# Evenly spread projection matmuls and an earlier path for the softmax reciprocals in a gated cross-attention kernel

## The chip, the cores and the metric

The kernel runs on one core of a Trainium2 chip. The metric is the device time of one execution in microseconds (us). A core has a matmul engine (PE, with its weight loads shown as PEld), a vector engine (DVE), a scalar engine (ACT), GpSimd (POOL), and SyncE (SP), which here only issues DMA transfers. Each engine runs its own instruction stream in order and waits on semaphores for the others. ACT also issues some DMAs, from the same instruction stream as its arithmetic.

## What is computed

For x and ctx of shape (8, 512, 512), 16 heads of 32, a mask over keys and two gates:

```
Q = layernorm(x) Wq' + bq,  K = ctx Wk' + bk,  V = ctx Wv' + bv
attn = softmax(where(mask, -1e9, Q K' / sqrt(32)))          # per head, 512 x 512
x1 = x + tanh(g_xattn) * ((attn V) Wo' + bo)
h = layernorm(x1);  h_prev = h shifted by one row
xr, xk = mur*h + (1-mur)*h_prev,  muk*h + (1-muk)*h_prev
out = x1 + tanh(g_ffn) * sigmoid(xr Wr') * (relu(xk Wk2')^2 Wv2')
```

Projections are computed in three matmul terms (high x low, low x high, high x high) of float32 split in two parts.

## The kernel before

**Two stages.** Stage 1 computes attention for 8 batches and writes the context to DRAM; stage 2 (from about 850 us) is the output projection and the gated feed-forward. The change touches stage 1 only.

**Groups and steps.** A batch has four groups of four heads, c = 0 to 3. A group has 16 tiles (head, 128 queries), one per step. At step i, PE does the scores of tile i + 2 (`scores`, one matmul of 512 columns), then this step's part of a projection (`side`), then four transposes of the probabilities of tile i (`transpose_probs`). DVE adds the mask and takes the row extreme of tile i + 2 (`mask_and_min`), ACT exponentiates tile i + 1 (`exp`). The transposed probabilities are copied out of PSUM by DVE at even and by ACT at odd steps (`probs_out`). After step 15 comes a last projection part (step 16), the scores of tile 18, and then `context`: 16 x 4-head matmuls that multiply all the transposed probabilities of the group with V.

**Projections.** Each group carries three projections of later groups (K, Q or V of some n), cut in parts over the steps by the table `PE_SIDE` (L57). K and Q have 12 matmuls of 512 columns, V has 24 of 256. The parts have 3 such matmuls (K, Q) or 4 (V), and three steps of each group have none: 2, 11 and 15 for c = 0; 2, 13 and 15 for c = 1; 10, 11 and 15 for c = 2; 6, 11 and 15 for c = 3. ACT takes the high part of a finished K or Q from PSUM (`HI_SIDE`) at the step after its last part, DVE the rest (`LO_SIDE`) one step later. SP stores both to DRAM, and loads the K and Q of the next group back in another layout (`load_bands`, L371: six loads of 256 KB, `k_stack` and `q_stack`). These loads are issued early in each group, after context has begun, or in c = 2 just before.

**Reciprocals.** The context must be divided by the sums of the exponentials. At the end of a group DVE takes their reciprocals (`rden`). PE transposes them into a side bank (item "R", L523) after `context`. DVE copies this out at step 2 of the next group (L929), ACT stores it to DRAM (`store_rden`, L749, 8 KB) after step 4, and reads it back spread over partitions in two halves after steps 6 and 8 (`spread_rden`, L754, two DMAs each). `spread_rden` first waits, on ACT, for the landing of the store. DVE divides at step 11 (`divide`, L945), and SP stores the result (`store_context`) and, in c = 0, then loads the next batch's ctx (`load_ctx`, 1 MB).

**Other DMAs from ACT** (`prepare`): rows of x for the statistics (`load_rows`, c = 3, steps 0, 2, 10, 12), columns of x (`load_xT`), and store and spread of the means and deviations (`store_mean_rstd`, `spread_mean_rstd`).

In this text "the group at 414.0" is the stretch from one context product, at 414.0 us, to the next; its steps belong to c = 3. Those at 439.9, 464.8 and 488.8 belong to c = 0, 1 and 2.

Of the kernel before, what the change touches and what calls it, by code (L numbers as in the profile page):

```python
# [25 lines left out]
P = 128  # L26
# [21 lines left out]
TERMS = 3  # L48
# [3 lines left out]
def parts(kind, n, *steps):  # L52
# [10 lines left out]
PE_SIDE_FIRST = [  # L63
    parts("K", 1, 0, 1, 2, 3) | parts("K", 2, 5, 6, 7, 8) | parts("V", 1, 9, 10, 11, 12) | parts("Q", 2, 13, 14, 15, 16),
# [3 lines left out]
def out_side(pe_side, lag, r_step):  # L68


    table = [{} for _ in range(GROUPS)]
    for c in range(GROUPS):
        for step, items in pe_side[c].items():
            for kind, n, part, of in items:
                if part == of - 1:
                    at = step + 1 + (lag if kind != "V" else 0)
                    table[c].setdefault(at if at < TILES else END, []).append((kind, n))
        table[c][r_step] = [("R", (c - 1) % GROUPS)] + table[c].get(r_step, [])
    return table


def prepare_at(nb):

    first, then = nb - 2, nb - 1
    if nb == 1:
        return {(0, 0, 0): ("xT", 0), (0, 0, 2): ("xT", 1), (0, 0, 14): ("store", 0), (0, 1, 1): ("spread", 0),
                (0, 1, 14): ("xT", 2), (0, 2, 0): ("xT", 3)}
    return {(first, 3, 0): ("rows", 0), (first, 3, 2): ("rows", 1), (first, 3, 10): ("rows", 2),
            (first, 3, 12): ("rows", 3), (first, 3, 14): ("xT", 0), (then, 0, 2): ("xT", 1), (then, 0, 12): ("store", 0),
# [3 lines left out]
def stats_at(nb):  # L93
# [5 lines left out]
HI_STEP, LO_STEP, DIVIDE_STEP = 1, 2, 11  # L99
RDEN_STORE, RDEN_SPREAD = 4, (6, 8)  # L100
HI_SIDE, LO_SIDE = ([out_side(pe_side, lag, step) for pe_side in (PE_SIDE_FIRST, PE_SIDE)]
                    for lag, step in ((0, HI_STEP), (1, LO_STEP)))
# [10 lines left out]
SIDE_BANKS = 3  # L113

SM_RING, P_RING, S_BANKS = 4, 4, 2
# [15 lines left out]
def build(nc, x, ctxT, mask, g_xattn, g_ffn, wq, bq, wk, bk, wv, bv, wo, bo, wr, wkk, wvv, mur, muk, ident_d, xT_d, out,  # L131
# [11 lines left out]
    with keep:  # L143
# [145 lines left out]
        def listed(table, b, c, step):  # L289

            return [i for i in table[min(b, 1)][c].get(step, []) if not (is_last(b) and i[:2] in NEXT_BATCH)
                    and not (c == 0 and i[:2] == ("R", GROUPS - 1))]
# [179 lines left out]
        def _(pe):  # L472
# [12 lines left out]

            def side(b, kind, n, part, of):
# [9 lines left out]
                if (kind, n) == ("Q", 4):  # L496
                    pe.wait_ge(x_lo, b * CH + part + 1)
                if (kind, n) == ("K", 4):
                    pe.wait_ge(ct_lo, b * CH + part + 1)
# [4 lines left out]
                if kind in "QK":  # L504
# [3 lines left out]
                    share = TERMS * CH // of  # L508
                    for at in range(part * share, (part + 1) * share):
# [3 lines left out]
                if kind == "V":  # L513

                    share = 2 * TERMS * CH // of
                    for at in range(part * share, (part + 1) * share):
# [12 lines left out]
            def scores(b, c, i):  # L529
# [9 lines left out]
                nc.tensor.matmul(s_bank[i % S_BANKS][:], stack[slot][0][:, j, q * P:(q + 1) * P],  # L539
# [23 lines left out]
            for kind, n in PROLOGUE:  # L563
                if (kind, n) == ("Q", 1):
                    scores(0, 0, 0)
                    scores(0, 0, 1)
# [3 lines left out]
            scores(0, 0, 2)  # L570

            def batch(b):
                for c in range(GROUPS):
                    for i in range(TILES):
                        if i and not (is_last(b) and c == GROUPS - 1 and i + 2 >= TILES):
                            scores(b, c, i + 2)
# [9 lines left out]
                    else:  # L586
                        scores(b, c, TILES + 2)
                    context(b, c)
                    side(b, "R", c, 0, 1)
# [86 lines left out]
        def _(act):  # L676
# [85 lines left out]
            def exp(b, c, i):  # L762
                if i == TILES:
# [15 lines left out]
            for kind, n in PROLOGUE:  # L779
# [5 lines left out]
                if (kind, n) == ("Q", 1):  # L785
                    exp(0, 0, 0)
# [514 lines left out]
```

## Time and profile before

| | us |
|---|---|
| median of 3 runs | 1232.18 (1228.26 to 1235.88) |
| the profiled execution | 1232.97, span 1230.7 |
| PE busy | 1149.9 (93%) |
| PEld busy | 902.0 (73%) |
| DVE busy | 902.8 (73%) |
| ACT busy | 697.8 (57%) |
| POOL busy | 352.2 (29%) |

In rows of the timeline, the columns are start (us), length (us), engine, line, operation, the tiles it writes and reads, shape and count; in brackets the idle time of the engine ahead of it and what ended it. "ACTq" and "SPq" are DMAs issued by that engine. A matmul's length contains its latency, so the time that PE spends on a step is read from start to start.

### The profile page before, as it was taken

To read this page: it belongs to the slowest core of one execution; us is meant where nothing else is said; L and a number is where in the kernel's file an instruction comes from. 1 tells how busy PE (TensorE), PEld (TensorE's weight loads), DVE (VectorE), ACT (ScalarE), POOL (GpSimd) and SP (SyncE) were. 2 spreads that over 40 slices of the span, in tenths; PEclk is the share of its full clock that TensorE was granted. 3 is DMA by queue.
4 is the path that set the end of the run, shared out by engine and by line. 5 is a ranking of instruction groups with operands and counts; after the bars stand their busy time and mean duration, and the time that the engine had idled before them with its cause. 6 is when DMAs were issued, how large, how long until landed. Compare 5 with 4: busy or idle time off the path is not lost.

```text
span 1230.7 us, 21575 instructions
## 1 busy us (share of the span) xinstructions
PE 1149.9 (93%) x7216; PEld 902.0 (73%) x7216; DVE 902.8 (73%) x1955; ACT 697.8 (57%) x1531; POOL 352.2 (29%) x574
## 2 busy tenths in 40 slices
PE   3999999999999899999999999987999999999997
PEld 3777677677667676767767777754888888888886
DVE  5767777788777787777767777879677677777763
ACT  4567677677666677667756776764432333233232
POOL 2134035035015214303502600024423433332431
PEclk9999999999999999999999999987999999999999
DMA  7674564774566458466457445642111211311200
GB/s 253 181 201 126 160 183 115 192 198 131 145 182 180 128 157 232 124 170 188 115 161 204 132 129 156 159 162 83 61 52 66 90 52 52 104 52 52 95 26 35
DMA packets 95644, 162.47 MB, mean 132 GB/s; under 512 B 13232, under 2 KB 22576, under 8 KB 95408
## 3 DMA queue, kind: packets, MB, share of 16 engines
q1 hardware_dynamic: 77968, 135.11, 38.5%
q10 hardware_dynamic: 17568, 26.00, 7.7%
q8 instruction: 59, 0.97, 0.3%
q14 instruction: 49, 0.40, 0.1%
HBM read 109.91 MB, written 49.57 MB: 130 GB/s over the span
## 4 chain that ended last, share of the span: by engine, by line
PE 72%; DMA 7%; issue 7%; DVE 6%; ACT 5%; ACTq 2%; SPq 1%; POOL 0%; POOLq 0%; DVEq 0%
PE bank L477 24%; PE bank L546 14%; PE bank L511 11%; PE bank L558 9%; PE bank L539 6%; DMA rden_dram<-ctx_sb 6%; PE bank L520 5%; DVE neg_s L958 2%; ACT probs L769 2%; ACTq L759 2%; PE bank L613 1%; DVE xh L1066 1%; DMA pT<-wkT 1%; SPq L348 1%; ACT kact_hi L864 1%
## 5 line engine op out<-in xcount | busy, mean ns | idle before, releaser
L769 ACT ACTIVATE probs<-neg_s,negmax 128x512 f32<-128x512 f32 x512 | 367.9, 720 | 94.5 <-DVE negmax L958 71.4
L958 DVE CUSTOM_DVE_ANT_0 neg_s<-bank,mask_big 128x512 f32<-128x512 f32 x512 | 346.2, 681 | 22.3 <-PE bank L539 18.1
L546 PE MATMUL bank<-ident,probs 128*128 128x128 f32 x2048 | 317.2, 278 | 35.1 <-ACT probs L769 33.4
L546 PEld LDWEIGHTS bank<-ident,probs 128*128 128x128 f32 x2048 | 242.2, 142 | 97.0 <-ACT probs L769 65.6
L964 DVE COPY pT<-bank 128x512 f32<-128x512 f32 x256 | 176.4, 689 | 148.3 <-PE bank L546 147.4
L539 PE MATMUL bank<-k_stack,q_stack 96*128 96x512 f32 x512 | 243.6, 476 | 7.1 <-DVE negmax L958 4.3
L776 ACT COPY pT<-bank 128x512 f32<-128x512 f32 x256 | 148.8, 581 | 145.3 <-PE bank L546 141.7
L558 PE MATMUL bank<-pT,v_sb 128*32 128x512 f32 x1024 | 118.4, 603 | 1.8 <-issue 1.6
L539 PEld LDWEIGHTS bank<-k_stack,q_stack 96*128 96x128 f32 x512 | 97.7, 191 | 11.5 <-DVE negmax L958 6.2
L862 ACT ACTIVATE relu<-bank 128x512 f32<-128x512 f32 x32 | 19.2, 598 | 149.3 <-PE bank L477 149.3
L769 ACT ACTIVATION_READ_ACCUMULATOR probs<-neg_s,negmax 128x1 f32 x512 | 97.2, 190 | 0.0
L1172 POOL COPY mean_rstd<-mv 128x4 f32<-128x4 f32 x7 | 1.3, 186 | 305.6 <-DVE mv L914 269.7
L1242 POOL TENSOR_TENSOR o_sb<-o_sb,x 128x1024 f32<-128x1024 f32 x16 | 39.1, 2442 | 173.5 <-DVE o_sb L1125 173.5
L558 PEld LDWEIGHTS bank<-pT,v_sb 128*32 128x32 f32 x1024 | 32.6, 111 | 70.1 <-issue 70.1
L1178 POOL TENSOR_TENSOR x_rows<-x_rows 128x512 f32<-128x512 f32 x28 | 35.6, 1282 | 153.5 <-DMA x_rows<-mr_dram 96.2
L511 PE MATMUL bank<-cT_lo,wk_hi 128*128 128x512 f32 x128 | 53.5, 418 | 16.9 <-DVE cT_lo L933 16.9
L1227 POOL TENSOR_TENSOR x_in<-x_in,tgbo 128x1024 f32<-128x1024 f32 x16 | 39.0, 2439 | 103.0 <-DMA x_in<-x 102.0
L511 PE MATMUL bank<-xT_lo,wq_hi 128*128 128x512 f32 x128 | 53.3, 416 | 1.8 <-DVE xT_lo L937 1.5
L1110 DVE TENSOR_TENSOR kact_lo<-kact,kact_hi 128x1024 fp32r<-128x1024 f32 x16 | 40.4, 2526 | 17.9 <-ACT kact_hi L864 17.9
L511 PE MATMUL bank<-cT_hi,wk_lo 128*128 128x512 f32 x128 | 52.1, 407 | 0.0
L511 PE MATMUL bank<-cT_hi,wk_hi 128*128 128x512 f32 x128 | 52.0, 406 | 0.0
L1050 DVE SCALAR_TENSOR_TENSOR x<-bank,tg,x_in 128x512 f32<-128x512 f32 x32 | 23.9, 750 | 37.4 <-POOL o_sb L1242 35.8
(119 smaller groups left out, 2129.7 us busy)
## 6 DMA issues: line engine op xcount, KB each, us to landing
q_stack<-qk_dram SPq DMA_DIRECT2D x93, 256.0 KB, 6.5
k_stack<-qk_dram SPq DMA_DIRECT2D x93, 256.0 KB, 5.2
cT_raw<-ctxT SPq DMA_DIRECT2D x8, 1024.0 KB, 7.0
rden_bc<-rden_dram ACTq DMA_DIRECT2D x128, 64.0 KB, 2.0
ctx_dram<-ctx_sb SPq DMA_DIRECT2D x32, 256.0 KB, 3.1
c_raw<-ctx_dram SPq DMA_DIRECT2D x16, 512.0 KB, 4.9
x_in<-x SPq DMA_DIRECT2D x16, 512.0 KB, 6.3
out<-o_sb SPq DMA_DIRECT2D x16, 512.0 KB, 3.3
```

What stands on the lines that cost most here:

```text
L477: mm = nc.tensor.matmul(dst, lhs(left, a), rhs(right, a), start=(part == 0 and a == 0), stop=(part == TERMS - 1 and a == CH - 1))
L511: mm = nc.tensor.matmul(bank[:], left[:, at // TERMS, cols], right[:, at // TERMS, :], start=(at == 0), stop=(at == TERMS * CH - 1))
L520: mm = nc.tensor.matmul(bank[:, k * UNIT:(k + 1) * UNIT], left[:, a, keys * P:(keys + 1) * P], right[:, a, n // 2 * UNIT:(n // 2 + 1) * UNIT],
L539: nc.tensor.matmul(s_bank[i % S_BANKS][:], stack[slot][0][:, j, q * P:(q + 1) * P], stack[slot][1][:, j, :], start=True, stop=True).then_i ...
L546: mm = nc.tensor.transpose(pt_bank[i % 2][:, a * P:(a + 1) * P], probs[:, i % P_RING, a * P:(a + 1) * P], ident[:])
L558: mm = nc.tensor.matmul(pv_bank[j * HD:(j + 1) * HD, :], v_sb[:, a, head * HD:(head + 1) * HD], pT[:, j, a, :], start=(a == 0), stop=(a == ...
L769: nc.scalar.activation(probs[:, i % P_RING, :], neg_s[:, i % SM_RING, :], ACT.Exp, bias=negmax[:, k:k + 1], scale=-1.0, accum_out=den[:, g ...
L776: nc.scalar.copy(pT[:, j, :, q * P:(q + 1) * P], blocks(pt_bank[i % 2])).then_inc(pt_out[1], 1)
L958: nc.vector.tensor_tensor_reduce(neg_s[:, i % SM_RING, :], s_bank[i % S_BANKS][:], mask_big[:, q, :], 1.0, 3e38, ALU.add, ALU.min, negmax[ ...
L964: nc.vector.tensor_copy(pT[:, j, :, q * P:(q + 1) * P], blocks(pt_bank[i % 2])).then_inc(pt_out[0], 1)
L1110: nc.vector.tensor_tensor(kact_lo[:].rearrange("p a t -> p (a t)"), kact[:].rearrange("p m d -> p (m d)"), kact_hi[:].rearrange("p a t -> ...
L1242: nc.gpsimd.tensor_tensor(o_sb[:, h], o_sb[:, h], x1[:, h], ALU.add).then_inc(o_done, 1)
```

## The change

The projections are cut in 6, 6 and 5 parts (in the first group 4, 4, 4 and 5), so that every step 0 to 16 has one; parts of K and Q have 2 or 3 matmuls, of V 4 or 5. At a step ACT and DVE do their tile work (`exp`, `mask_and_min`) ahead of the projection results. PE transposes the reciprocals ahead of `context`, DVE copies them at the end of the same group, ACT stores them after step 1 and spreads them after steps 5 and 7, and DVE divides after step 10. Loads of one part of x and the store of the means move by one or two steps. Constants get names (AHEAD_S, AHEAD_P); those edits generate the same instructions.

```
 PE_SIDE = [
-    parts("K", 2, 0, 1, 3, 4) | parts("V", 1, 5, 6, 7, 8, 9, 10) | parts("Q", 2, 12, 13, 14, 16),
-    parts("Q", 3, 0, 1, 3, 4) | parts("K", 3, 5, 6, 7, 8) | parts("V", 2, 9, 10, 11, 12, 14, 16),
-    parts("V", 3, 0, 1, 2, 3, 4, 5) | parts("Q", 4, 6, 7, 8, 9) | parts("K", 4, 12, 13, 14, 16),
-    parts("V", 0, 0, 1, 2, 3, 4, 5) | parts("K", 5, 7, 8, 9, 10) | parts("Q", 5, 12, 13, 14, 16),
+    parts("K", 2, *range(0, 6)) | parts("V", 1, *range(6, 12)) | parts("Q", 2, *range(12, 17)),
+    parts("Q", 3, *range(0, 6)) | parts("K", 3, *range(6, 12)) | parts("V", 2, *range(12, 17)),
+    parts("V", 3, *range(0, 6)) | parts("Q", 4, *range(6, 12)) | parts("K", 4, *range(12, 17)),
+    parts("V", 0, *range(0, 6)) | parts("K", 5, *range(6, 12)) | parts("Q", 5, *range(12, 17)),
 ]
-            (first, 3, 12): ("rows", 3), (first, 3, 14): ("xT", 0), (then, 0, 2): ("xT", 1), (then, 0, 12): ("store", 0),
+            (first, 3, 12): ("rows", 3), (first, 3, 14): ("xT", 0), (then, 0, 3): ("xT", 1), (then, 0, 10): ("store", 0),
-HI_STEP, LO_STEP, DIVIDE_STEP = 1, 2, 11
-RDEN_STORE, RDEN_SPREAD = 4, (6, 8)
+DIVIDE_STEP = 10
+RDEN_STORE, RDEN_SPREAD = 1, (5, 7)
...
+            def share(total, part, of):
+                return range(total * part // of, total * (part + 1) // of)
...
                         scores(b, c, TILES + 2)
+                    side(b, "R", c, 0, 1)
                     context(b, c)
-                    side(b, "R", c, 0, 1)
...
             def tile_step(b, c, i):
+                if not (is_last(b) and c == GROUPS - 1 and i + AHEAD_P >= TILES):
+                    exp(b, c, i + AHEAD_P)
                 for kind, n in listed(HI_SIDE, b, c, i):
                     side(b, kind, n)
-                if not (is_last(b) and c == GROUPS - 1 and i + 1 >= TILES):
-                    exp(b, c, i + 1)
...
             def tile_step(b, c, i):
+                if not (is_last(b) and c == GROUPS - 1 and i + AHEAD_S >= TILES):
+                    mask_and_min(b, c, i + AHEAD_S)
                 for kind, n in listed(LO_SIDE, b, c, i):
                     side(b, kind, n)
-                if not (is_last(b) and c == GROUPS - 1 and i + 2 >= TILES):
-                    mask_and_min(b, c, i + 2)
...
                     for kind, n in listed(LO_SIDE, b, c, END):
                         side(b, kind, n)
+                    if not (is_last(b) and c == GROUPS - 1):
+                        side(b, "R", c)
```

## Rows read from the trace of the kernel before

**Rows 1.** Windows: us, busy us (instructions) per engine, PE clock, DMA share, GB/s
```profile
414.00:439.90 25.90, 23.59 (x162) 17.72 (x161) 19.31 (x48) 17.26 (x43) 0.00 (x0) 1.00 0.65 172
439.90:464.80 24.90, 23.93 (x162) 17.84 (x161) 19.48 (x52) 17.44 (x43) 3.15 (x16) 1.00 0.61 152
464.80:488.80 24.00, 23.89 (x162) 17.78 (x161) 18.39 (x47) 17.91 (x44) 11.61 (x11) 1.00 0.83 241
488.80:513.10 24.30, 23.23 (x165) 18.06 (x164) 18.24 (x46) 16.94 (x42) 12.99 (x14) 1.00 0.38 99
...
311.50:339.60 28.10, 25.22 (x162) 18.94 (x161) 19.37 (x48) 17.50 (x43) 0.00 (x0) 0.94 0.59 160
...
sum 603.00, PE 571.88 PEld 432.68 DVE 452.75 ACT 417.46 POOL 166.48; mean PE 95.31 PEld 72.11 DVE 75.46 ACT 69.58 POOL 27.75
```

**Rows 2.** Timeline of PE in the group at 414.0 (c = 3)
```profile
413.98 3.64 PE L558 MATMUL bank<-pT,v_sb 128*32 128x512 f32 x32
...
418.15 0.60 PE L546 MATMUL bank<-ident,probs 128*128 128x128 f32 x4
...
419.33 0.60 PE L546 MATMUL bank<-ident,probs 128*128 128x128 f32 x4
...
423.93 0.60 PE L546 MATMUL bank<-ident,probs 128*128 128x128 f32 x4
...
424.60 0.60 PE L546 MATMUL bank<-ident,probs 128*128 128x128 f32 x4
...
429.70 0.66 PE L546 MATMUL bank<-ident,probs 128*128 128x128 f32 x4 [2.18 <-ACT probs L769]
...
431.12 0.60 PE L546 MATMUL bank<-ident,probs 128*128 128x128 f32 x4
...
432.48 0.60 PE L546 MATMUL bank<-ident,probs 128*128 128x128 f32 x4
...
438.39 0.66 PE L546 MATMUL bank<-ident,probs 128*128 128x128 f32 x4
```

**Rows 3.** Timeline of PE, one row in c = 3, one in c = 2
```profile
327.80 0.66 PE L546 MATMUL bank<-ident,probs 128*128 128x128 f32 x4 [2.76 <-ACT probs L769]
...
506.80 0.66 PE L546 MATMUL bank<-ident,probs 128*128 128x128 f32 x4 [1.06 <-ACT probs L769]
```

**Rows 4.** Timeline of ACT and its DMAs in the group at 414.0
```profile
422.48 0.33 ACTq L751 DMA_DIRECT2D rden_dram<-ctx_sb  x1
...
427.92 0.81 ACTq L759 DMA_DIRECT2D rden_bc<-rden_dram  x2
428.83 0.72 ACT L769 ACTIVATE probs<-neg_s,negmax 128x512 f32<-128x512 f32 x1 [2.96 <-DVE negmax L958]
```

**Rows 5.** ACT's load of x, and all DMA queues from 420.5 to 424.0 us
```profile
420.13 0.36 ACTq L713 DMA_DIRECT2D x_rows<-x  x1
...
q1 hardware_dynamic: 436, 0.79, 105.6%
```

**Rows 6.** Last stack load of four groups: its issue, then us to landing
```profile
419.68 0.43 SPq L379 DMA_DIRECT2D k_stack<-qk_dram  x1
...
k_stack<-qk_dram SPq DMA_DIRECT2D x1, 256.0 KB, 7.7
...
445.24 0.43 SPq L379 DMA_DIRECT2D q_stack<-qk_dram  x1
...
q_stack<-qk_dram SPq DMA_DIRECT2D x1, 256.0 KB, 7.4
...
470.70 0.43 SPq L379 DMA_DIRECT2D q_stack<-qk_dram  x1
...
q_stack<-qk_dram SPq DMA_DIRECT2D x1, 256.0 KB, 7.0
...
218.54 0.43 SPq L379 DMA_DIRECT2D k_stack<-qk_dram  x1
...
k_stack<-qk_dram SPq DMA_DIRECT2D x1, 256.0 KB, 7.3
```

More of the change, by code:

```diff
@@ L96, in stats_at @@
         (nb - 2, 3, 7), (nb - 2, 3, 9), (nb - 1, 0, 3), (nb - 1, 0, 5))
-HI_STEP, LO_STEP, DIVIDE_STEP = 1, 2, 11
-RDEN_STORE, RDEN_SPREAD = 4, (6, 8)
-HI_SIDE, LO_SIDE = ([out_side(pe_side, lag, step) for pe_side in (PE_SIDE_FIRST, PE_SIDE)]
-                    for lag, step in ((0, HI_STEP), (1, LO_STEP)))
+DIVIDE_STEP = 10
+RDEN_STORE, RDEN_SPREAD = 1, (5, 7)
+HI_SIDE, LO_SIDE = ([out_side(pe_side, lag) for pe_side in (PE_SIDE_FIRST, PE_SIDE)] for lag in (0, 1))
 C_ITEMS, T_ITEMS = [("C", n) for n in range(CH)], [("T", n) for n in range(TT)]
@@ L289, in listed @@
         def listed(table, b, c, step):
-            return [i for i in table[min(b, 1)][c].get(step, []) if not (is_last(b) and i[:2] in NEXT_BATCH)
-                    and not (c == 0 and i[:2] == ("R", GROUPS - 1))]
+            return [i for i in table[min(b, 1)][c].get(step, []) if not (is_last(b) and i[:2] in NEXT_BATCH)]
         def is_last(b):
@@ L496, in side @@
                 if (kind, n) == ("Q", 4):
-                    pe.wait_ge(x_lo, b * CH + part + 1)
+                    pe.wait_ge(x_lo, b * CH + (share(CH * TERMS, part, of)[-1]) // TERMS + 1)
                 if (kind, n) == ("K", 4):
-                    pe.wait_ge(ct_lo, b * CH + part + 1)
+                    pe.wait_ge(ct_lo, b * CH + (share(CH * TERMS, part, of)[-1]) // TERMS + 1)
                 if kind == "T":
@@ L507, in side @@
                     w_hi, w_lo, r_hi, r_lo = w1_hi[which], w1_lo[which], act_hi[which], act_lo[which]
-                    share = TERMS * CH // of
-                    for at in range(part * share, (part + 1) * share):
+                    for at in share(TERMS * CH, part, of):
                         left, right = ((w_hi, r_lo), (w_lo, r_hi), (w_hi, r_hi))[at % TERMS]
@@ L513, in side @@
                 if kind == "V":
-                    share = 2 * TERMS * CH // of
-                    for at in range(part * share, (part + 1) * share):
+                    for at in share(2 * TERMS * CH, part, of):
                         k, term, a = at // (TERMS * CH), at // CH % TERMS, at % CH
@@ L538, in scores @@
                 pe.wait_ge(s_min, tile_no(b, c, i) + 1)
-                nc.tensor.matmul(s_bank[i % S_BANKS][:], stack[slot][0][:, j, q * P:(q + 1) * P],
+                nc.tensor.matmul(s_bank[tile_no(b, c, i) % S_BANKS][:], stack[slot][0][:, j, q * P:(q + 1) * P],
                                  stack[slot][1][:, j, :], start=True, stop=True).then_inc(s_mm, 1)
@@ L564, in _ @@
                 if (kind, n) == ("Q", 1):
-                    scores(0, 0, 0)
-                    scores(0, 0, 1)
+                    for i in range(AHEAD_S):
+                        scores(0, 0, i)
                 if kind in "KQV":
@@ L569, in _ @@
                 side(None, kind, n, 0, 1)
-            scores(0, 0, 2)
+            scores(0, 0, AHEAD_S)
             def batch(b):
@@ L574, in batch @@
                     for i in range(TILES):
-                        if i and not (is_last(b) and c == GROUPS - 1 and i + 2 >= TILES):
-                            scores(b, c, i + 2)
+                        if i and not (is_last(b) and c == GROUPS - 1 and i + AHEAD_S >= TILES):
+                            scores(b, c, i + AHEAD_S)
                         for item in listed(PE_SIDES, b, c, i):
@@ L762, in exp @@
             def exp(b, c, i):
-                if i == TILES:
+                if i == TILES and b * GROUPS + c:
                     act.wait_ge(rden_ready, b * GROUPS + c + HEAD)
@@ L785, in _ @@
                 if (kind, n) == ("Q", 1):
-                    exp(0, 0, 0)
+                    for i in range(AHEAD_P):
+                        exp(0, 0, i)
                 if (kind, n) == ("Q", 0):
@@ L985, in _ @@
                     dve.wait_ge(mask_done, 1)
-                    mask_and_min(0, 0, 0)
-                    mask_and_min(0, 0, 1)
+                    for i in range(AHEAD_S - 1):
+                        mask_and_min(0, 0, i)
                 if (kind, n) == ("Q", 0):
```

19 lines of the change are left out of this document (9 added, 10 removed).

## Prediction

> **What bounds the kernel now.** I read first the shares of busy time (PE 93%, the others 73% or less), then the windows of single groups, then the timelines of PE and ACT inside a group. Six batches in the steady part take 603.0 us, 100.5 each [rows 1]. The four groups of the batch that begins at 414.0 take 25.9, 24.9, 24.0 and 24.3 us for nearly the same matmuls, so something other than PE's work separates them [rows 1].
>
> Read PE's steps from one group of transposes to the next [rows 2]. A step with a V part takes 1.18 us (418.15 to 419.33), one with three K or Q matmuls 1.36 (431.12 to 432.48), one with nothing 0.67 (423.93 to 424.60). So a K or Q matmul costs 0.23 us and four V matmuls about 0.5. The first transposes come 4.17 us after the context product starts [rows 2].
>
> PE stands still in two places. In c = 3 it idles 2.18 us (2.76 in an earlier batch) ahead of the transposes of step 8 [rows 2, 3]. ACT shows why: the store of the reciprocals is issued at 422.48, and the wait for its landing holds ACT until 427.92; only then do the spreads start, the next exponential at 428.83, and PE's transposes at 429.70, 1.8 us after the release [rows 2, 4]. The row of the exponential names DVE as releaser, but between it and that idle time stand the spreads, so the real cause is the DMA. In c = 2, PE idles 1.06 us at step 12 [rows 3]: steps 10 and 11 have no projection part, PE runs through them in 0.67 us each, and the exponentials (0.72 us on ACT and the DVE work ahead of them) can't follow.
>
> Why does an 8 KB store take 5.4 us (422.48 to 427.92)? From 420.5 to 424.0 only SP's queue moved data, at 105.6% of the 16 engines' time, although ACT's load of x had been issued at 420.13 [rows 5]. So what is issued later waits until everything issued before it has drained, whichever queue it is on. The last stack load, issued at 419.68, landed 7.7 us later, at 427.38 [rows 6], and the store half a microsecond after it, with the load of x between.
>
> **Even parts.** PE's work is unchanged; only its place moves. With T the start of a step's transposes counted from the start of context, the new group has T(0) = about 4.0 (4.17 less a little, since R's short transposition now stands ahead), steps of 2 x 0.23 + 0.67 = 1.13 or about 1.16 with V, so T(7) = 4.0 + 7 x 1.15 = 12.05. From T(7) to the next context: four steps more of 1.15 (4.6), steps 12 to 15 with 2, 2, 3, 2 matmuls (3 x 1.13 + 1.36 = 4.75), and 1.53 for the end (438.39 to 439.92, [rows 2] and the window's edge at 439.9) plus 0.15 for R: 11.05. A group without a stall takes 23.1 us. In c = 2 the stall goes: 24.3 to 23.1, a gain of 1.2 [rows 1, 3]. Its reciprocals are no trouble, since its stack loads start ahead of context.
>
> **Tile work first.** Same instructions in another order on ACT and DVE; both have slack (17 to 19 us busy of 24 to 26, [rows 1]). The price is that a finished projection is taken out up to one exponential (0.72, [rows 4]) later; the next user of that bank is six steps away. Cost 0.
>
> **R ahead of context.** PE now waits for DVE's reciprocals before context instead of after. DVE makes them while PE does part 16 and the last scores, about 0.9 us. I take 0; if that cover fails, up to the one exponential of 0.72 per group. The copy on DVE moves into context's 3.64 us [rows 2], in which DVE waits for PE: 0. The means are stored two steps earlier, after a chain on POOL that I bound by one step (0 to 1.15, once a batch): I take 0.
>
> **Store and spread: here I expect no gain.** The store moves from after step 3's copy to after step 1's, two PE steps: to about 5.9 us after the start of context (was 8.5: 422.48 less 413.98, [rows 2, 4]). But the last stack load is issued at 5.7, 5.3 and 5.9 us in the groups c = 3, 0 and 1 (419.68, 445.24, 470.70 less 413.98, 439.9, 464.8; [rows 1, 6]), so it is still ahead, and the store lands just behind it, which I take as 0.2 us. What changes is that the load of x (c = 3 and 0) is no longer ahead. The spread, however, is now waited for after step 5, ahead of exp(7), where it was after step 6, ahead of exp(8). So the exponential that is late is needed one step earlier, and PE stalls at step 7: T(7) = landing of the last load + 0.2 + 1.8.
>
> - c = 3: landing 427.38 less 413.98 = 13.4; T(7) = 15.4; group 15.4 + 11.05 = 26.4 (was 25.9): +0.5. PE idles about 3.15 us (15.4 less 12.05 less 0.2 of modelled latency).
> - c = 0: landing 452.64 less 439.9 = 12.7; T(7) = 14.7. Here a Q or K high part (as an exponential, 0.72) stands on ACT right behind exp(7), which costs some 0.5 more over the next two steps. 14.7 + 11.05 + 0.5 = 26.3 (was 24.9): +1.4.
> - c = 1: landing 477.70 less 464.8 = 12.9. The 1 MB load of ctx ahead of it starts about 1 to 1.5 us earlier, since the division moves up; I take 1.0 (bounds 0 and 1.5), so 11.9. T(7) = 13.9; group 25.4 (was 24.0): +1.4. Before, PE reached step 8 just as late as the exponential, and nothing was lost.
> - c = 2: -1.2.
>
> Sum: +2.1 us for this batch. **The clock** comes on top. Where PE idled 2.76 us the granted clock of the window is 0.94 and the group took 28.1; where it idled 2.18 the clock stayed at 1.00 and it took 25.9 [rows 1 to 3]. 0.94 is a mean over stretches at the full 2.4 GHz and at 1.2 GHz; less 0.6 for the longer idle time, the fall costs 1.6 us. The new 3.15 us in c = 3 is beyond 2.76, so +1.6: this batch goes from 99.1 to 102.8.
>
> The Trainium skill (TensorE: Matmul & The Clock Gate, HAM oscillation) also says that gaps in PE's work throttle it again and names waits on DMAs as the typical cause; the trace agrees, with 0.94 against 1.00.
>
> This batch's loads land late: in the group at 213.4 the last one lands at 218.54 + 7.3 less 213.4 = 12.4, one microsecond sooner than 13.4 [rows 6]. I take off half of that in c = 3 and in c = 0: 101.8 as the mean of the new batches, against 100.5: +1.3, six times about +8. Outside these six, the last batch has no loads of x that could leave the way, so its c = 3 and c = 0 groups lose about 1 to 2 us each, its c = 2 and the first batch's win 1.1 each: +1. Stage 2 is unchanged. The profiled execution (1232.97) becomes 1242; it stands 0.8 above the median of the runs, so **1241**.
>
> **Rivals.**
> - *Stalls move, little changes* (the above): 1225 to 1250. For it: the silence of ACT's queue while SP's drains [rows 5]. Against: it rests on landings within 0.2 us of each other.
> - *The store doesn't wait for the loads.* Then it lands within some 2 us, before step 5 ends; all stalls go, every group takes 23.1 to 23.3 us, a batch 92.8. 100.5 less 92.8 = 7.7, six times 46, with the ends 49: 1184. Against it stands the load of x at 420.13 that moved nothing for 3.9 us [rows 5].
> - *The store overtakes the last stack load* (5.9 against an issue at 5.3 to 5.9 us): lands one load (1.2 us) sooner, in up to 3 groups of a batch, and the clock mostly stays up. 3.6 x 7 = 25 less than the forecast: 1216.
> - *Slower: the clock falls in c = 0 and 1 too.* It decides from an idle time of between 2.18 and 2.76 us [rows 2, 3]; c = 0 has 14.7 less 12.25 = 2.45. Two more falls of 1.6 in seven batches: +22, 1263.
>
> The second rival would follow from the Trainium skill (DMA: Bandwidth & Descriptors, Queues, rings and completion order): each DMA engine takes turns between the queues that have work, packet by packet, so a short store on ACT's queue would not stand behind SP's megabytes. By that rule the kernel would take 1184; the trace of before disagrees, with q1 alone at 105.6% of the engines' time.
>
> **How the numbers follow.** Forecast 0.53, no wait behind the loads 0.15, overtaking 0.12, clock falls 0.20. A measurement of this kernel tells about 1% from no change. Faster by over 1% (below 1220): 0.15 + 0.12 = 0.27. Slower (over 1244.5): 0.20 and a fifth of the forecast's share, 0.10: 0.30. Within 1%: 0.43. The range reaches from overtaking with its own margin (1205) to the clock falls (1267); the forecast alone is 1225 to 1250.
>
> **What would show it.** Right: in c = 3, 0 and 1 the spread starts 12 to 14 us after context does, just after the last stack load lands, though the store is issued near 5.9; PE idles 1.5 to 3 us at step 7 and no longer at step 8; c = 2 takes 23.1 us; half-clock stretches in most c = 3 groups. Wrong: landings of the store well ahead of the last load; spread issued right after step 5's copy; all groups near 23.1; or idle time of PE ahead of context, where R waits.

## The result and the profile after

| | us |
|---|---|
| changed kernel, median of 20 runs | 1242.68 (1233.96 to 1250.22) |
| kernel before, median of 20 runs beside them | 1232.11 (1226.66 to 1236.65) |
| ratio, 95% interval | 1.008 (1.0059 to 1.010) |
| span of the profiled execution | 1240.8 (before 1230.7) |

The change costs 0.8%: the interval lies above 1, and the size is within the 1% that the prediction called no change. The forecast was 1241.

Below, T(n) is the start of the transposes of step n, counted from the start of the context product, as in the prediction. The windows of the same batch as in [rows 1], group by group (c = 3, 0, 1, 2), and the sum over the six steady batches:

```profile
418.00:443.20 25.20, 23.61 (x162) 17.64 (x161) 19.51 (x48) 17.66 (x43) 0.00 (x0) 1.00 0.61 165
443.20:470.20 27.00, 24.99 (x165) 19.33 (x164) 19.60 (x52) 17.79 (x43) 3.16 (x16) 0.94 0.66 191
470.20:495.50 25.30, 23.63 (x166) 17.60 (x168) 18.81 (x47) 18.16 (x44) 12.29 (x11) 1.00 0.63 179
495.50:519.10 23.60, 23.55 (x165) 17.60 (x164) 18.06 (x46) 16.81 (x42) 12.29 (x14) 1.00 0.45 110
...
sum 607.50, PE 575.30 PEld 433.78 DVE 456.15 ACT 421.67 POOL 166.45; mean PE 95.88 PEld 72.30 DVE 76.03 ACT 70.28 POOL 27.74
```

Six batches take 607.5 us instead of 603.0 [rows 1]. In this batch c = 3 and c = 2 became shorter (25.9 to 25.2, 24.3 to 23.6), c = 0 and c = 1 longer; on the mean of the six batches only c = 2 did. The other three are still 1.6 to 3.4 us longer than c = 2. I call them blocked: in them ACT, at the spreads, stands waiting for the landing of the store.

The timeline of PE in the second of these groups shows where it stands still (compare [rows 2, 3]):

```profile
443.23 3.64 PE L557 MATMUL bank<-pT,v_sb 128*32 128x512 f32 x32
...
447.37 0.60 PE L545 MATMUL bank<-ident,probs 128*128 128x128 f32 x4
...
454.19 0.60 PE L545 MATMUL bank<-ident,probs 128*128 128x128 f32 x4
...
457.51 0.66 PE L545 MATMUL bank<-ident,probs 128*128 128x128 f32 x4 [2.01 <-ACT probs L768]
...
458.81 1.09 PE L545 MATMUL bank<-ident,probs 128*128 128x128 f32 x4
```

Steps 0 to 6 run through evenly: 6.82 us for six steps, 1.14 each. Then PE idles 2.01 us ahead of step 7, not of step 8 as before. The row after it is the clock: the four transposes that took 0.60 now take 1.09, and the window's granted clock is 0.94.

Why step 7 is late stands in the timeline of ACT and its DMAs (compare [rows 4]):

```profile
449.15 0.33 ACTq L750 DMA_DIRECT2D rden_dram<-ctx_sb  x1
...
455.73 0.81 ACTq L758 DMA_DIRECT2D rden_bc<-rden_dram  x2
456.64 0.72 ACT L768 ACTIVATE probs<-neg_s,negmax 128x512 f32<-128x512 f32 x1 [2.37 <-DMA rden_dram<-ctx_sb]
```

SP's own timeline has the stack loads issued just ahead of that store (compare [rows 6]):

```profile
448.11 1.26 SPq L377 DMA_DIRECT2D q_stack<-qk_dram  x3
```

And the view of the DMA queues from 449.2 to 452.5 us gives packets, MB and share of 16 engines for each queue, then size and us to landing of what was issued (compare [rows 5]):

```profile
q1 hardware_dynamic: 371, 0.67, 99.7%
q10 hardware_dynamic: 4, 0.00, 0.2%
...
q_stack<-qk_dram SPq DMA_DIRECT2D x1, 256.0 KB, 6.6
...
rden_dram<-ctx_sb ACTq DMA_DIRECT2D x1, 8.0 KB, 6.6
```

The store goes out at 449.15, 5.9 us after context starts, nearly 3 us sooner than before. It lands 6.6 us later, near 455.7, just behind the last stack load (issued near 448.9, also 6.6). From 449.2 to 452.5 one queue moved 99.7% and the other 0.2% of what 16 engines can. ACT sends the spreads at 455.73, the exponential follows at 456.64, and PE starts again at 457.51: 1.8 us after the landing, as before. This time the idle row of the exponential names the DMA itself.

The page of the profile says the same of the whole execution: in the chain of work that ended last, the store of the reciprocals (`rden_dram<-ctx_sb`) has grown from 6% to 10%.

Of the span's 10.1 us, 4.5 are in the six batches, and 4.1 more are in a single place. The group c = 2 of the last batch went from 21.7 to 25.8 us; its window:

```profile
793.40:819.20 25.80, 21.60 (x142) 15.78 (x142) 17.52 (x45) 16.31 (x41) 0.00 (x0) 0.87 0.61 158
```

PE's timeline at its step 7:

```profile
807.56 1.11 PE L545 MATMUL bank<-ident,probs 128*128 128x128 f32 x4 [2.77 <-ACT probs L768]
```

And what SP had issued ahead of its reciprocals:

```profile
791.73 0.46 SPq L392 DMA_DIRECT2D w_raw<-woT  x1
792.29 2.07 SPq L377 DMA_DIRECT2D k_stack<-qk_dram  x3
794.45 1.58 SPq L377 DMA_DIRECT2D q_stack<-qk_dram  x3
```

SP's rows in the same place before, where that group starts at 786.06:

```profile
782.35 0.44 SPq L394 DMA_DIRECT2D w_raw<-woT  x1
782.89 1.69 SPq L379 DMA_DIRECT2D k_stack<-qk_dram  x3
784.67 1.88 SPq L379 DMA_DIRECT2D q_stack<-qk_dram  x3
```

A 1 MB load of weights for the next stage stands ahead of the stack loads in both kernels. Before, the loads were all issued ahead of context, the store behind them landed 10.7 us after its start, and ACT first waited for it at 10.8: nothing was lost. Now the last three are issued 1.1 to 2.0 us after it, the store lands at 12.4, as late as elsewhere in c = 3, and ACT waits for it from step 5 on. Step 7 waits 2.77 us, and the clock falls to 0.87. The loads come later because of the even parts: SP issues them behind the store of K, whose last part moved from step 8 to step 11 of the group before. The kernel with the even parts alone has the late landing too (12.1, and 22.6 us for the group), and the kernel with the rest of the change and the old parts has not (10.0, and 22.6 us).

### The profile page after: what moved, and what is told of

Same layout as the page of the kernel before. It is cut to its first block, busy times and chain, and to the rows that moved or that the text cites. A ratio compares the mean times of both kernels' runs of the same rounds, so it can differ in the third digit from the quotient of the medians.

```text
span 1240.8 us, 21575 instructions
## 1 busy us (share of the span) xinstructions
PE 1155.4 (93%) x7216; PEld 904.4 (73%) x7216; DVE 906.7 (73%) x1955; ACT 702.9 (57%) x1531; POOL 352.4 (28%) x574
## 4 chain that ended last, share of the span: by engine, by line
PE 74%; DMA 11%; issue 6%; DVE 3%; ACT 2%; ACTq 2%; SPq 1%; POOL 0%; POOLq 0%; DVEq 0%
PE bank L475 24%; PE bank L545 15%; PE bank L511 11%; DMA rden_dram<-ctx_sb 10%; PE bank L557 9%; PE bank L538 7%; PE bank L519 6%; ACTq L758 1%; PE bank L612 1%; SPq L346 1%; DVE xh L1067 1%; DMA pT<-wkT 1%; ACT probs L768 1%; DVE neg_s L958 1%; ACT kact_hi L864 1%
## 5 line engine op out<-in xcount | busy, mean ns | idle before, releaser
L545 PE MATMUL bank<-ident,probs 128*128 128x128 f32 x2048 | 321.2, 281 | 42.0 <-ACT probs L768 41.4
L545 PEld LDWEIGHTS bank<-ident,probs 128*128 128x128 f32 x2048 | 247.4, 143 | 111.8 <-ACT probs L768 75.8
L538 PE MATMUL bank<-k_stack,q_stack 96*128 96x512 f32 x512 | 247.5, 484 | 8.0 <-DVE negmax L958 5.6
L538 PEld LDWEIGHTS bank<-k_stack,q_stack 96*128 96x128 f32 x512 | 99.7, 195 | 10.4 <-DVE negmax L958 6.8
L511 PE MATMUL bank<-xT_hi,wq_lo 128*128 128x512 f32 x128 | 51.2, 400 | 0.0
```

The costliest lines, as they stand in the source:

```text
L511: mm = nc.tensor.matmul(bank[:], left[:, at // TERMS, cols], right[:, at // TERMS, :], start=(at == 0), stop=(at == TERMS * CH - 1))
L538: nc.tensor.matmul(s_bank[tile_no(b, c, i) % S_BANKS][:], stack[slot][0][:, j, q * P:(q + 1) * P], stack[slot][1][:, j, :], start=True, st ...
L545: mm = nc.tensor.transpose(pt_bank[i % 2][:, a * P:(a + 1) * P], probs[:, i % P_RING, a * P:(a + 1) * P], ident[:])
```

## The experiments

All twelve are variants of the changed kernel or of the one before. Each ran beside the kernel before on its chip (medians 1228.3 to 1229.6), so ratios are compared. The first three (even parts alone, store after step 4, store after step 1) and the change itself make a ladder from the kernel before to the changed one.

### Even parts alone

The kernel before with the new tables of parts (and their shares of matmuls), nothing else (one row of the table shown):

```diff
-    parts("K", 2, 0, 1, 3, 4) | parts("V", 1, 5, 6, 7, 8, 9, 10) | parts("Q", 2, 12, 13, 14, 16),
+    parts("K", 2, *range(0, 6)) | parts("V", 1, *range(6, 12)) | parts("Q", 2, *range(12, 17)),
...
```

> The kernel before with the even parts alone; reciprocals, spreads and the order on ACT and DVE as before. Theory: c = 2 loses its stall (23.1 us); in the others T(8) = landing of the store (as before, 13 to 14 us) + 1.8, and the rest of the group takes 9.9 us: 25.6, 25.1 and 24.7 us for c = 3, 0 and 1, with a few half-clock stretches 99.3 for a batch against 100.5: 7 us faster than the kernel before. Rival (even parts remove PE's waits for ACT in general): all groups near 23.1, 40 us faster.

Measured: 1222.9 us, ratio 0.9963 (0.9938 to 0.9988). The window of c = 2:

```profile
486.10:509.40 23.30, 23.17 (x164) 17.75 (x163) 18.06 (x46) 16.93 (x42) 11.67 (x13) 1.00 0.40 103
```

c = 2 takes 23.3, nearly the predicted 23.1. In c = 3 the stall at step 8 stays; the even parts are worth about 5 us, near the 7 expected.

### The waits back at steps 6 and 8, the store at step 4 and at step 1

Two kernels: the changed one with the store, the spreads and the division where they were before (so even parts, tile work first, R ahead and the moved loads of x remain), and the same with the store after step 1 (`RDEN_STORE` 1 again).

```diff
-DIVIDE_STEP = 10
-RDEN_STORE, RDEN_SPREAD = 1, (5, 7)
+DIVIDE_STEP = 11
+RDEN_STORE, RDEN_SPREAD = 4, (6, 8)
```

Store after step 4:

> The kernel spread_6_8 with the store back after step 4, so what the earlier store is worth where the spreads are after steps 6 and 8. Theory (strict order of issue): in c = 3 and 0 the load of x is ahead of the store again, the landing and T(8) 0.6 to 1.4 us later, in c = 1 unchanged: about 1 us in two groups of a batch plus a half-clock stretch or two, 12 to 18 us slower than spread_6_8, 1205 to 1211. Rival (the earlier store is of use by itself): c = 1 later as well, 1215 or more.

Store after step 1:

> The changed kernel with the spreads back after steps 6 and 8 and the division after step 11; the store stays after step 1. Theory (the store lands just behind the last stack load, and what counts is which exponential stands behind the wait): the landing stays at 11.2 to 13 us after the start of context, but the late exponential is that of step 8, so T(8) is landing + 1.8 where it is now T(7). Each blocked group (3 of 4, 23 in all) gets 1.2 us shorter, minus 26 us, and most half-clock stretches go, 5 of 1.6 us: about 1208 us. Rival (the wait costs what the store takes, wherever it is waited for): about 1242, as the changed kernel.

Measured: 1213.17 us, 0.9875 (0.9834 to 0.9915), and 1193.17 us, 0.9711 (0.9661 to 0.976). The windows c = 3, 0, 1, 2 of the latter:

```profile
396.30:420.50 24.20, 23.40 (x162) 17.79 (x161) 19.31 (x48) 17.48 (x43) 0.00 (x0) 1.00 0.66 175
420.50:444.20 23.70, 23.35 (x166) 17.92 (x165) 19.36 (x52) 17.75 (x43) 3.19 (x16) 1.00 0.73 200
444.20:468.50 24.30, 23.55 (x162) 17.49 (x161) 18.67 (x47) 18.02 (x44) 12.82 (x12) 1.00 0.70 198
468.50:491.50 23.00, 23.00 (x162) 17.89 (x161) 18.02 (x46) 16.73 (x42) 11.83 (x13) 1.00 0.45 114
```

The batch takes 95.2 instead of 101.1 us. So the earlier store is worth 20 us as long as the wait for it stays where it was, and moving the wait one step forward (with the division after step 10 instead of 11) takes 49.5 us by the medians and 45 by the ratios: all that the other edits had won, and more.

Both are more than I expected (12 to 18 us, and 34). Of the first, c = 1 has its part too, which strict order did not give: 23.9 to 23.6 on the mean of six batches. The second can be taken apart in the timelines of PE. In the blocked groups the store lands at about the same time and PE starts 1.8 us later in both kernels; but from T(7) to the next context the changed kernel takes 11.3 us (without a fall of the clock), and from T(8) this one takes 9.9. That is 1.4 us in each of 23 groups, 32 us: the step between, 1.14 us, and 0.2 of what the place of the spreads costs (see below). Seven falls of the clock are gone, some 10 us. And c = 2, where ACT waits in neither, went from 23.6 to 23.0: 4 us in seven groups. That is 46 of the 47 us between the spans of the two profiles (1240.8 and 1193.6). The ladder:

| kernel | ratio |
|---|---|
| before | 1 |
| + even parts | 0.9963 |
| + tile work first, R ahead, loads of x moved | 0.9875 |
| + store after step 1 | 0.9711 |
| + spreads after 5 and 7 (the change) | 1.008 |

### The waits even later

Spreads after steps 8 and 10, division after 13:

```diff
-DIVIDE_STEP = 10
-RDEN_STORE, RDEN_SPREAD = 1, (5, 7)
+DIVIDE_STEP = 13
+RDEN_STORE, RDEN_SPREAD = 1, (8, 10)
```

> The changed kernel with the spreads after steps 8 and 10 and the division after step 13. Theory: the wait is reached at about 13 us, when the store has landed or nearly, so that no group stalls; all groups take 23.6 to 23.7 us as c = 2 does now, 94.5 for a batch instead of 101.2; with the ends about 1195 us. Rival (a later division holds up the store of the context, the load of the next ctx and with it the stack loads of c = 1, or DVE waits for the spread rows): gain half of that or less, 1215 or more.

Measured: 1190.68 us, 0.9704 (0.9665 to 0.9743), not to be told from the previous one by the intervals. The stalls are gone: no wait of PE for an exponential is over 0.7 us, and the groups are 23.3 to 23.9 us. But c = 2, which had no stall to lose, went from 23.0 to 23.4 on the mean. The price is at the end of the group. With the division after step 13, DVE makes the reciprocals later, and PE, with R ahead of context, waits for them: from the last scores to context it takes 0.7 to 0.8 us (once 1.2) where it took 0.44; only at the end of c = 0 it stays 0.44.

### The stack loads later

If the store stands behind the stack loads, letting SP send these five tiles later must free it, with the spreads still after steps 5 and 7:

```diff
-                sp.wait_ge(s_mm, (g - 1) * TILES + HEAD)
+                sp.wait_ge(s_mm, (g - 1) * TILES + HEAD + 5)
```

(The division is after step 13.)

> The changed kernel, store and spreads as they are, but SP issues the six stack loads of a group only once the scores of its tile 4 are done, so behind the store of the reciprocals; the division is after step 13, since the spread rows now stand behind the loads. Theory (strict order of issue across the queues): the store, with nothing ahead, lands 1.4 to 2 us after its issue, as it does in c = 2 of the kernel before, near 7.5 us; no wait at step 5; groups near 23.7, about 1195 us, unless the loads, which now land near 19 us, are late for the scores of step 14. Rival (a slow store has other reasons than the loads ahead): latency stays at 5 to 7 us and the time at 1242.

Measured: 1199.29 us, 0.9771 (0.9734 to 0.9808). The row of the store's line, its time to landing over all 32 groups, of the changed kernel and of this one:

```profile
DMA to landing us min/median/max: 1.3/5.7/7.8
```

```profile
DMA to landing us min/median/max: 1.3/1.4/5.1
```

Same store, same queue, same 8 KB, same time of issue: median 5.7 us behind the stack loads, 1.4 ahead of them. The store is no longer among the lines of the page's chain, where it had 10%. This is the theory of the prediction, shown by changing what stands ahead. The later division, the other edit of this kernel, is not what frees the store: the kernel with spreads after 8 and 10 has it too, and there the median is 5.9 us.

Still, its c = 2 group takes 23.8 us and not 23.1. The timeline of ACT at the first spread:

```profile
480.16 0.81 ACTq L758 DMA_DIRECT2D rden_bc<-rden_dram  x2
481.07 0.72 ACT L768 ACTIVATE probs<-neg_s,negmax 128x512 f32<-128x512 f32 x1 [0.38 <-DVE negmax L958]
```

No landing is waited for here, but issuing two spreads takes ACT 0.8 us, and the exponential that PE needs next, that of tile 7, stands behind them. So next came the same loads with the spreads after steps 6 and 8:

> The kernel loads_later with one edit: the spreads after steps 6 and 8 instead of 5 and 7. In neither does ACT wait for the store, so this measures the place alone. Theory: ACT's copy of the transposed probabilities is at the odd steps and waits for PE; a spread right behind it keeps the next exponential back just when PE needs it (T(7) 12.3 to 12.4 and 1.3 at step 9 in loads_later), while behind an even step the next exponential is already on its way: T(7) 12.1, 0.4 to 0.5 us less in each of 31 groups, 1199 becomes about 1185. Rival (the place doesn't matter without a wait): 1199.

Measured: 1183.71 us, 0.9644 (0.9622 to 0.9667). The same place on ACT:

```profile
471.14 0.33 ACTq L758 DMA_DIRECT2D rden_bc<-rden_dram  x1
471.38 0.73 ACT L768 ACTIVATE probs<-neg_s,negmax 128x512 f32<-128x512 f32 x1
471.50 0.45 ACTq L758 DMA_DIRECT2D rden_bc<-rden_dram  x1
```

and the windows of c = 0 and 2:

```profile
413.90:437.10 23.20, 23.20 (x164) 17.95 (x163) 19.30 (x52) 17.23 (x43) 3.15 (x16) 1.00 0.65 161
...
460.40:483.70 23.30, 23.16 (x162) 17.87 (x161) 17.91 (x46) 16.61 (x42) 11.67 (x13) 1.00 0.46 114
```

After step 6 the exponential of tile 7 stands ahead of the spreads in ACT's program, with no copy of probabilities between; it starts between the two issues and isn't held up. That is worth 15.6 us, 0.5 us in each of 31 groups, as expected (1185). All four groups of a batch now take 23.2 to 23.6 us. Below I call this kernel the unblocked one.

### Spreads after steps 4 and 6

With the store landing at 7.3 us, the spreads could go sooner. Loads six tiles later, then nine, spreads after 4 and 6, division after 10:

> A version meant to beat both: the changed kernel with the stack loads held until the scores of tile 5 are done, the spreads after the even steps 4 and 6, the division after step 10. Theory: the store lands at 7.3 us, ACT never waits for it, and at even steps the spreads don't hold up the next exponential that PE needs (spread_6_8 had 23.0 us in c = 2, where the changed kernel has 23.6): all groups 23.0 to 23.2 us, about 1175. Rival (the stack loads, now landing at 17 to 20 us, are late for the scores of step 14): stalls at the end of the group, 1190 or more.

> The kernel spread_4_6_loads_later with one edit: the stack loads wait for the scores of tile 8, so that they stand behind both spreads, not only the store. Theory: the spread rows land 2 us after their issue, the division at step 10 no longer waits (39.7 us in 30 waits in spread_4_6_loads_later), groups 23.0 to 23.2 us, about 1175. The loads are issued from 11 us on and land at 18.5 to 20 after the start of context, and the scores of step 14 need them at 20. Rival (they are late in c = 1 or 0, where K or Q wait for their own stores, or in c = 0 behind the load of x): a new stall at step 14, 1190 to 1230.

Both missed: 1234.64 us, 1.0067 (1.0029 to 1.0105), and 1229.74 us, 1.0003 (0.9986 to 1.0021). With six tiles, who waits for the second spread is DVE; the rows of its division:

```profile
its engine sat idle before it (us, times) until:
  DMA rden_bc<-rden_dram: 39.7, 30
```

The second spread (after step 6) was issued behind the first stack loads, the division came after step 10, and DVE stood 1.3 us on the mean of 30 waits. The row minima queue behind it, and PE's scores wait for them at step 13: 43.2 us in 32 waits, most of the loss. With nine tiles, the stack loads themselves are late, and PE's scores wait for them, 20.3 us in 23 waits:

```profile
487.44 0.50 PE L538 MATMUL bank<-k_stack,q_stack 96*128 96x512 f32 x1 [1.49 <-DMA q_stack<-qk_dram]
```

That is not all of it: c = 0, at 26.0 us on the mean, lost most (23.2 in the unblocked kernel). There a second wait for a landing in ACT's program fell behind the loads, that for the store of the means:

```profile
366.09 0.72 ACT L768 ACTIVATE probs<-neg_s,negmax 128x512 f32<-128x512 f32 x1 [3.35 <-DMA mr_dram<-mean_rstd]
```

ACT's last copy of probabilities comes after it, and PE's context product stands 1.7 us for it. In effect SP's and ACT's transfers go as one queue here, and whatever is put last in it needs a late reader. Loads five tiles later, spreads after 6 and 8 and the division after 13 leave slack on both sides; these leave none.

### The order inside a step

Side work (the high and low parts of a finished projection) back ahead of the exponential and the row minimum, in the changed kernel and in the unblocked one:

```diff
-                if not (is_last(b) and c == GROUPS - 1 and i + AHEAD_P >= TILES):
-                    exp(b, c, i + AHEAD_P)
                 for kind, n in listed(HI_SIDE, b, c, i):
                     side(b, kind, n)
+                if not (is_last(b) and c == GROUPS - 1 and i + AHEAD_P >= TILES):
+                    exp(b, c, i + AHEAD_P)
```

(and likewise on DVE)

> The changed kernel with ACT and DVE taking out finished projections ahead of the tile work again, as before. Theory A (the prediction's term: the order costs nothing): 1242 within 3. Theory B: in c = 0 and 1 the high part of a projection (0.6 us on ACT) now stands between the released wait and exp(7), so T(7) is landing + 2.4 there instead of 1.8: plus 0.6 less what it cost behind exp(7) (0.2 to 0.4), times 14: 1245 to 1250.

> The kernel with the stack loads five tiles later and the spreads after steps 6 and 8 (1183.7 us), with only the order inside a step turned back: on ACT the high part of a finished projection ahead of the exponential, on DVE the low part ahead of the row minimum. Nothing in this kernel holds ACT for a landing. Theory A (the order inside a step matters only where a stall has used up the lead of the exponentials, as in the changed kernel, where turning it back cost 15 us): 1184 to 1188, and no group longer than 24. Theory B (the order costs by itself, an exponential of 0.72 us late each time a projection is finished, some three times in a group): 0.3 to 0.5 us in most of the 31 groups, 1193 to 1200, with PE's idle time in front of the transposes that follow a finished projection.

Measured: 1258.21 us, 1.0263 (1.0213 to 1.0313), against 1242.7; and 1189.59 us, 0.9699 (0.9664 to 0.9734), against 1183.7. The timeline of ACT in a c = 0 group of the blocked kernel:

```profile
365.90 0.81 ACTq L758 DMA_DIRECT2D rden_bc<-rden_dram  x2
366.83 0.69 ACT L705 ACTIVATE k_hi<-bank,bk_col 128x512 fp32r<-128x512 f32 x1 [2.50 <-DMA rden_dram<-ctx_sb]
367.42 0.71 ACT L768 ACTIVATE probs<-neg_s,negmax 128x512 f32<-128x512 f32 x1
```

PE in the same place:

```profile
368.28 0.90 PE L545 MATMUL bank<-ident,probs 128*128 128x128 f32 x3 [2.71 <-ACT probs L768]
```

and the window of that group:

```profile
353.30:382.20 28.90, 26.19 (x162) 20.56 (x161) 19.72 (x52) 17.79 (x43) 3.18 (x16) 0.88 0.59 164
```

The first instruction after the release is the high part, and the exponential comes 0.6 us later: 2.4 us from release to PE instead of 1.8, and the clock falls. The second theory had this, but not its size: it expected 1250 at most, and the falls of the clock, on which it had put nothing, add to it (c = 0 is 27.2 on the mean of six batches, from 26.1). In the unblocked kernel c = 0 and 1 take 23.7 (from 23.2 and 23.3), the others stay. So both theories of that run hold in part: the order costs by itself, 6 to 7 us, and the stalls make 15 to 22 of it (medians, ratios).

### Uneven parts with the rest of the change

```diff
-    parts("K", 2, *range(0, 6)) | parts("V", 1, *range(6, 12)) | parts("Q", 2, *range(12, 17)),
+    parts("K", 2, 0, 1, 3, 4) | parts("V", 1, 5, 6, 7, 8, 9, 10) | parts("Q", 2, 12, 13, 14, 16),
...
```

> The changed kernel with the uneven parts of the kernel before. Theory: with parts of three matmuls PE reaches step 7 of c = 1 only at 13.2 us, about when exp(7) comes anyway, so c = 1 needs no stall (23.9 us); c = 0 24.9; c = 3 26.1 and half-clock stretches; c = 2 has its old stall (24.3): 99.9 for a batch against 101.2 of the changed kernel, 8 us faster than that, about 1231. Rival (even parts are what gains in this change and the rest loses): slower than the changed kernel, 1250.

Missed: 1242.06 us, 1.0106 (1.0061 to 1.0152), the same as the change within the intervals. The windows of c = 1 and 2:

```profile
473.90:498.80 24.90, 24.17 (x162) 17.85 (x161) 18.77 (x47) 18.36 (x44) 9.96 (x9) 1.00 0.75 200
498.80:522.70 23.90, 23.39 (x162) 17.93 (x161) 17.90 (x46) 16.79 (x42) 14.63 (x15) 1.00 0.37 94
```

Where a landing sets T(7), it does not matter how PE spends the steps before it. I had expected c = 1 to need no stall, but PE idled 0.1 to 1.1 us at its step 7 in every one of the six batches. The equal totals are a sum of unequal parts: on the mean of six batches the old parts are 0.3 us longer in c = 1 and in c = 2 and 1.1 shorter in c = 0, the last c = 2 takes 22.6 us instead of 25.8, and in this profile the first context starts 5 us later, which I can't explain. So the even parts are worth 5 us with the spreads after step 6, and nothing clear of noise with the spreads after step 5.

### R behind the context product

The unblocked kernel with the short transposition of the reciprocals back in its old place:

```diff
-                    side(b, "R", c, 0, 1)
                     context(b, c)
+                    side(b, "R", c, 0, 1)
```

> The same kernel (1183.7 us) with only the short transposition of the reciprocals put back behind the context product on PE. The prediction costed its move at nothing, with up to 0.72 us in a group if DVE's reciprocals were late for PE. Theory A (no cost and no gain by itself; the store goes out at the same point or up to 0.5 us later, still ahead of the stack loads, and lands in time for step 6): 1182 to 1186, store landed by 8 us after the context product starts. Theory B (its place ahead of context costs, because PE waits there for DVE's reciprocals): turning it back gains 0.2 to 0.7 us in each of 31 groups, 1162 to 1178. Theory C (the place ahead of context is needed: behind it the store waits for PE's last context matmul and DVE's copy, gets behind the first stack loads, and blocks again): 1195 or more.

Measured: 1179.47 us (1178.41 to 1180.98), 0.9606 (0.9581 to 0.9632), the fastest kernel here; its interval just touches that of the unblocked one. PE around context at the end of c = 0 in the unblocked kernel, then in this one:

```profile
436.65 0.40 PE L538 MATMUL bank<-k_stack,q_stack 96*128 96x512 f32 x1
436.89 0.27 PE L524 MATMUL bank<-ident,rden 128*16 128x128 f32 x1
437.09 3.64 PE L557 MATMUL bank<-pT,v_sb 128*32 128x512 f32 x32
```

```profile
434.35 0.40 PE L538 MATMUL bank<-k_stack,q_stack 96*128 96x512 f32 x1
434.68 3.64 PE L557 MATMUL bank<-pT,v_sb 128*32 128x512 f32 x32
438.25 0.28 PE L524 MATMUL bank<-ident,rden 128*16 128x128 f32 x1
438.28 0.48 PE L511 MATMUL bank<-xT_lo,wq_hi 128*128 128x512 f32 x1
```

From the last scores to context it is 0.44 us with R between and 0.33 without; behind context R delays the next matmul by 0.03. At the end of the other three groups more is lost, since there R waits for DVE's reciprocals, which come late with the division after step 13; at the end of one c = 2 in the unblocked kernel:

```profile
390.13 0.27 PE L524 MATMUL bank<-ident,rden 128*16 128x128 f32 x1 [0.16 <-DVE rden L970]
```

There it is 0.7 to 0.8 us from the last scores to context, and 0.45 to 0.55 in this kernel. The store still goes out 6.0 us after context starts (5.9 before). So moving R ahead bought nothing. By these rows it costs 0.1 us a group by itself, and 0.2 in three of four groups where the division is late, which more than covers the measured 4.2 us, 0.14 in each of 31 groups. Theory B of this run held, at a price below the one it named.

## Why the prediction was right, and where not

**The landing rule held.** There are 23 blocked groups (c = 3, 0 and 1 throughout, and the last c = 2). In 19 of them T(7) is the landing of the store + 1.8, in the others + 1.9 to 2.0. The store lands 0.2 us behind the last stack load issued before it in 19; of the others one landed 0.2 ahead of a load that had been issued 0.2 before it, two 0.4 behind and one 1.35 behind. In c = 0 above, 12.5 + 1.8 = 14.3, measured 14.28. The loads sent later (5.7 to 1.4 us) show that it is the loads that hold the store. The rival in which the store passes them would have given 1184. The Trainium skill's rule for it (DMA: Bandwidth & Descriptors, Queues, rings and completion order: engines take turns between queues, packet by packet) isn't what this trace shows: one queue at 99.7%, the other at 0.2%. What keeps the store's data back is not shown, only the order in which things land.

**The stall moved from step 8 to step 7**, as forecast. Putting the wait back (45 to 50 us) shows that it is what made the kernel slower. R ahead adds little: 0.1 us a group where the division is early, as here.

**The sum was right by luck, by errors that cancel.** Forecast: +8 in the six steady batches, +1 at the ends. Measured: +4.5 and +5.6 (10.1 less 4.5). The terms, as means of the six batches (the forecast's means take 1.6 for the clock in c = 3, and half a microsecond off c = 3 and c = 0):

| group | before | forecast | measured |
|---|---|---|---|
| c = 3 | 26.8 | 27.5 | 26.8 |
| c = 0 | 25.2 | 25.8 | 26.1 |
| c = 1 | 24.3 | 25.4 | 24.7 |
| c = 2 | 24.2 | 23.1 | 23.6 |

- *c = 2, the unstalled group*: 23.1 forecast, 23.6 measured, because the spreads after an odd step cost 0.5 to 0.6. With the spreads after steps 6 and 8 and nothing else changed but the division it is 23.0. I had counted the wait for the spreads, and not their issue of 0.8 us.
- *c = 3*: its stall came as forecast, but the clock fell in three of six and not in all. In the batch shown it took 25.2, where 26.4 and a fall were forecast: its last stack load was issued behind the store (near 6.5 us), and the store landed at 12.1, one load sooner. This is the overtaking of the third rival, at its price of 1.2, but it happened in two of 31 groups and not in three of each batch.
- *c = 0*: 27.0 in the batch shown, with a fall of the clock, and 25.2 in a group without one. The forecast had no fall here and 0.5 for the high part behind exp(7). That 0.5 never came: from T(7) on, c = 0 takes 11.3 us as c = 3 and c = 1 do.
- *c = 1*: the forecast's own numbers give 13.9 + 11.05 = 24.95, not 25.4; the working doesn't say what the other 0.45 is. The last stack load lands at 11 to 11.6 and not at 11.9. The 25.3 of the batch shown is a coincidence: T(7) was 13.0, and PE waited another 0.93 us at step 9, behind a second pair of spreads of which one took 1.5 us to issue. The mean rose by 0.4 only, also since two of the six had lost 1.2 and 1.3 us at step 8 before; I had read one batch in which nothing was lost.
- *The last batch's c = 2*: forecast a gain of 1.1, measured a loss of 4.1. This was the step that failed most. "Its stack loads start ahead of context" was read from the kernel before and taken over unchanged, but the even parts finish K three steps later, and SP issues the loads behind K's store. The last of them is now issued 0.9 to 2.6 us after context starts in every c = 2 (0.2 to 1.3 before it, in the kernel before). In the steady batches the store still lands before ACT asks for it (7.9 to 9.9 us, against 10.6); in the last, behind the 1 MB of weights, it doesn't.

**The clock fell as often as forecast, in other places, which is luck too.** Forecast: most c = 3 groups. Measured: six falls in the six batches (three before), three in c = 3 and three in c = 0, and one in the last c = 2. The fourth rival had falls in c = 0, in addition to all of c = 3. The rule "it decides from an idle time of between 2.18 and 2.76 us" fell: the clock went down after 3.20 and 2.69 us, but also four times after 1.90 to 2.09, and stayed up after 2.42 and 2.44. The timeline of PE above (2.01 us, 0.94) is one; the window of a c = 3 group with the other, 2.44 idle at step 7:

```profile
318.10:344.50 26.40, 23.66 (x164) 17.68 (x163) 19.59 (x48) 17.58 (x43) 0.00 (x0) 1.00 0.61 158
```

That idle time matters at all holds: with the stalls gone, none of the first 30 groups of the unblocked kernel and its two variants has a window below 1.00. What else decides stays open.

**"Tile work first: cost 0"** had the right sign of the price and overlooked the gain: turned back it costs at least 15 us here, 6 without stalls. **"R ahead: 0"** is 4 us slower than R behind in the unblocked kernel, whose later division is part of that price, and within the bound given (0.72 a group).

## What to carry to other kernels

Ask of each wait on a DMA which compute instruction stands behind it on its engine, and when that one is needed: here the same wait one step sooner costs 45 to 50 us. Ask also what each edit does to the times at which the transfers are issued: the even parts moved the loads on which everything else was timed. In this kernel a small urgent transfer is as late as the bulk that was issued before it, on either queue; send the bulk after it, and let the reader of whatever is last come late. Judge such edits one by one: here three that gain 35 us together were hidden by a fourth that takes 45 to 50.

## What I had not expected of the hardware

- The issue of two transfers takes 0.8 us of ACT even if no landing is waited for. After a step with a copy of probabilities it costs PE 0.2 us at each of two steps, 0.5 a group in all; after one without, nothing (c = 2 takes 23.0 us).
- The clock fell after 1.90 us of idle time in one group and not after 2.44 us in another. One fall made a group with 14.3 us to step 7 take 27.0, where 14.3 and the usual 11.3 behind it make 25.6: 1.4 us, close to the 1.6 of the forecast. The dearest was in a window with a clock of 0.88, the first c = 3: 13.9 us behind step 7, 2.6 more.
- The order of issue holds across the two queues for spreads as for stores: with the loads six tiles later, the second spreads were those that stood behind them, and DVE waited 39.7 us in all for them.
